# Output projection two slots later, moments of x two slots earlier, batch 1's conv taps two slots later, and the last batch's y projected block by block

## What is computed

```python
# layer 0: Mamba block, d_inner 512, 16 states, conv of 4 taps
xn = layernorm(x) * (1 + scale) + shift
x_in, z = split(xn @ in_proj)
u = silu(conv4(x_in)); dt_r, B, C = split(u @ x_proj); dt = softplus(dt_r @ dt_proj + b)
h[t] = h[t-1] * exp(dt[t] * A) + (dt[t] * u[t]) * B[t]      # a scan over t for 512 x 16 rows
y = (sum_n h * C + u * D) * silu(z)
x = x + gate * (y @ out_proj)
# layer 1: linear attention, 8 heads of 32
q, k, v = rows of layernorm(x);  q = softmax over a head's 32;  k = softmax over time, masked
att = k^T v per head;  y = q att
x = x + silu(layernorm(y) * (1 + scale) + shift) @ W_out + b_out
```

## Time and profile before

| | |
|---|---|
| median of 3 runs | 592.57 us (592.15, 592.57, 598.32) |
| the profiled execution | 598.08 us, its span 596.3 us |
| VectorE busy | 525.1 us, 88% of the span |
| TensorE, GpSimd, ScalarE busy | 76%, 73%, 68% |
| mean granted TensorE clock | 0.86 |
| chain that ended last | VectorE 44%, GpSimd 17%, TensorE 15%, issue 13%, ScalarE 8% |

### The profile page before, as it was taken

The page is one execution under the profiler, slowest core; times in us unless marked ns, Lnnn a source line. Parts: engine busy times, 40 slices in busy tenths (PEclk is TensorE's granted clock), DMA queues, the critical chain, the costliest instruction groups (busy, mean ns, idle before and its releaser), DMA issues.

```text
span 596.3 us, 7355 instructions
## 1 busy us (share of the span) xinstructions
PE 455.0 (76%) x2445; PEld 370.4 (62%) x2445; DVE 525.1 (88%) x576; ACT 405.8 (68%) x885; POOL 436.2 (73%) x311
## 2 busy tenths in 40 slices
PE   8987756678677868779686868789776878657877
PEld 6656545457564757658574757667674767546755
DVE  2377999999999899999999999999999998899533
ACT  3673868588965977497856977497856976675242
POOL 4069779959976899577976899577977899683010
PEclk9977767889899788889789878879789877798988
DMA  9192034013310144003310143003300143000001
GB/s 269 50 353 59 18 143 140 3 28 125 125 35 1 38 168 124 1 27 127 125 52 1 44 162 124 0 28 143 124 35 10 34 153 117 1 18 1 0 1 36
DMA packets 22366, 45.38 MB, mean 76 GB/s; under 512 B 3684, under 2 KB 13556, under 8 KB 22328
## 3 DMA queue, kind: packets, MB, share of 16 engines
q1 hardware_dynamic: 22328, 44.92, 22.4%
HBM read 42.52 MB, written 2.39 MB: 75 GB/s over the span
## 4 chain that ended last, share of the span: by engine, by line
DVE 44%; POOL 17%; PE 15%; issue 13%; ACT 8%; DMA 2%; SPq 0%; DVEq 0%; ACTq 0%; POOLq 0%
DVE ring L855 22%; POOL hs L507 11%; DVE hs L855 6%; DVE hs L862 4%; DVE conv L830 4%; PE sums L1199 3%; ACT ring L667 3%; PE PY L1247 2%; POOL hs L516 2%; PE sums L1081 2%; DMA Br<-bc_rows 1%; PE PX L1147 1%; DVE st L810 1%; DVE ygT L869 1%; ACT L608 1%
## 5 line engine op out<-in xcount | busy, mean ns | idle before, releaser
L507 POOL TENSOR_TENSOR hs<-dtu,Br 128x1024 f32<-128x1024 f32 x127 | 296.3, 2359 | 8.9 <-DMA Br<-bc_rows 8.9
L667 ACT ACTIVATE ring<-dt,Aneg 128x256 f32<-128x256 f32 x512 | 213.1, 465 | 90.5 <-DVE hs L862 87.7
L855 DVE TENSOR_TENSOR_SCAN ring<-ring,hs 128x1024 f32<-128x1024 f32 x104 | 237.0, 2279 | 6.2 <-ACT ring L667 6.2
L1199 PE MATMUL sums<-ident,hs 128*128 128x128 f32 x1024 | 150.1, 303 | 37.1 <-DVE hs L862 36.9
L1199 PEld LDWEIGHTS sums<-ident,hs 128*128 128x128 f32 x1024 | 135.2, 159 | 53.0 <-DVE hs L862 49.1
L862 DVE TENSOR_TENSOR hs<-ring,Cr 128x1024 f32<-128x1024 f32 x104 | 127.3, 1224 | 3.6
L516 POOL TENSOR_TENSOR hs<-hs,Cr 128x1024 f32<-128x1024 f32 x24 | 56.6, 2358 | 56.1 <-DVE hs L855 56.1
L1247 PE MATMUL PY<-wqkvo,xT 128*128 128x256 f32 x168 | 57.8, 506 | 0.0
L855 DVE TENSOR_TENSOR_SCAN hs<-ring,hs 128x1024 f32<-128x1024 f32 x24 | 54.7, 2279 | 0.0
L1247 PEld LDWEIGHTS PY<-wqkvo,xT 128*128 128x128 f32 x168 | 44.9, 267 | 9.9
L591 ACT ACTIVATE conv<-PX,par 128x256 f32<-128x256 f32 x30 | 15.3, 559 | 52.1 <-PE PX L1147 51.9
(11 more groups left out here) (196 smaller groups left out, 670.4 us busy)
## 6 DMA issues: line engine op xcount, KB each, us to landing
Br<-bc_rows SPq DMA_DIRECT2D x32, 512.0 KB, 5.0
Cr<-bc_rows SPq DMA_DIRECT2D x32, 512.0 KB, 4.0
xg<-in_x SPq DMA_DIRECT2D x8, 256.0 KB, 2.8
out<-fin SPq DMA_DIRECT2D x7, 256.0 KB, 4.3
hs<-in_ada_wT SPq DMA_DIRECT2D x3, 512.0 KB, 4.7
win<-in_in_wT SPq DMA_DIRECT2D x2, 512.0 KB, 6.1
hs<-in_W_emb SPq DMA_DIRECT2D x2, 512.0 KB
gate<-gate_rows SPq DMA_DIRECT2D x8, 128.0 KB, 3.0
```

The lines of the kernel that those rows point to most:

```text
L507: nc.gpsimd.tensor_tensor(hs[:, g % DBUF], dtu[:, b % 2, dc, :].unsqueeze(1).to_broadcast([P, NQ, T]), Br[:, NQ * q:NQ * q + NQ, :], ALU.m ...
L667: ins = nc.scalar.activation(ring[:, g % 2, j, :], dt[:, b % 2, dc, :], ACT.Exp, scale=Aneg[:, c:c + 1])
L855: V.tensor_tensor_scan(driven if by_pool(g) else decays, decays, driven, 0.0, ALU.mult, ALU.add).then_inc(s_scan_done, 1)
L1199: ins = M(YT[:, c, :], hs[:, g % DBUF, j, P * c:P * c + P], ident[:, :], is_transpose=True, start=False, stop=(q == UPC - 1 and j == NQ - ...
```

## The change

It does five things, in the order of the program.

1. `conv_taps` 0 and 1 of batch 1 on VectorE, `conv_last_tap` 1 on ScalarE and `in_proj` 1, 2 and 3 on TensorE are due two slots later (`due_later`). All other batches keep their slots.
2. `stats0` is due in slot 7 of an earlier batch (-25) where it was in slot 9 (-23).
3. `output` is due in slot 7 (39), ahead of `x_proj`, where it was in slot 5 (37).
4. The last y is transposed back, copied and projected by blocks of 128 channels: blocks 0 to 2 during slots 10 to 15 (`last_back`, `last_yg`, `last_early`), through `PX`, and only block 3 after unit 127.
5. In the end part: VectorE does `last_x1` for both halves before batch 6's `head_blocks`, `normalize_q` and `stats2`; batch 6's attention on TensorE comes after the last projection of y; the transposed k goes to `PX` ahead of v and is copied by ScalarE; the head sums come after k times v; ScalarE's table load stands after the copy of q; batch 6's transposes move behind the head sums. GpSimd's queue is unchanged.

```diff
+def due_later(g, slot):
+    if g == U + slot + 2:
+        return 1
+    b = due(g, slot)
+    return None if b == 1 else b
...
+            def last_yg(dcs, bank):
+                n = len(dcs)
+                act.wait_ge(s_last_yback, dcs[-1] + 1)
+                act.wait_ge(s_out_mm, LAST_B)
+                nc.scalar.activation(yg[:, dcs[0]:dcs[0] + n, :], bank[:, 0:n, :], ACT.Copy).then_inc(s_last_yg, n)
+            def last_copy_kT():
+                act.wait_ge(s_kT_mm, NB)
+                nc.scalar.activation(kT[:, :, :], PX[:, :, :], ACT.Copy).then_inc(s_kT_ready, 1)
...
                 copy_kT(LAST_B - 1)
-                copy_yg(LAST_B)
+                last_yg((3,), z_bank(LAST_B))
                 last_normalize1(0)
-                normalize2(LAST_B - 1)
                 last_normalize1(1)
                 norm1(LAST_B)
+                normalize2(LAST_B - 1)
                 exp_k(LAST_B)
+                last_copy_kT()
                 exp_q(LAST_B)
-                nc.scalar.preload_act_table_set("silu_and_others")
                 mask_v(LAST_B)
                 copy_qT(LAST_B)
+                nc.scalar.preload_act_table_set("silu_and_others")
...
+                if g == LAST_B * U + 13:
+                    last_yg((0, 1), PX)
+                if g == LAST_B * U + 15:
+                    last_yg((2,), PX)
...
                 gate_y(LAST_B, DC - 1)
+                last_x1(0)
+                last_x1(1)
                 head_blocks(LAST_B - 1)
                 normalize_q(LAST_B - 1)
                 stats2(LAST_B - 1)
-                last_x1(0)
-                last_x1(1)
                 max_qk(LAST_B)
                 sum_k(LAST_B)
-                dve.wait_ge(s_kT_mm, NB)
-                V.tensor_copy(kT[:, :, :], y_bank(LAST_B)[:, :, :]).then_inc(s_kT_ready, 1)
...
-                for slot, step in ((-23, stats0), ...
+                for slot, step in ((-25, stats0), ...
-                    b = due(g, slot)
+                    b = (due_later if step in (conv_taps_0, conv_taps_1) else due)(g, slot)
...
+            def last_back(dcs, bank, until):
+                pe.wait_ge(s_ygT_ready, DC * LAST_B + until)
+                for i, dc in enumerate(dcs):
+                    for c in range(TC):
+                        ins = nc.tensor.transpose(bank[:, i, P * c:P * c + P], ygT[:, c, P * dc:P * dc + P], ident[:, :])
+                ins.then_inc(s_last_yback, len(dcs))
+            def out_part(c, dcs):
+                for k in dcs:
+                    ins = M(last_half(c), yg[:, k, P * c:P * c + P], wo[:, k, :], start=(k == 0), stop=(k == DC - 1),
+                            skip_group_check=True)
+                return ins
+            def last_early():
+                pe.wait_ge(s_last_yg, 3)
+                for c in range(TC):
+                    out_part(c, (0, 1, 2))
...
-                                   (-13, in_proj_3), (-9, x_proj), ...
+                                   (-13, in_proj_3), (39, output), (-9, x_proj), ...
-                                   (35, transpose_y), (37, output)):
-                    b = due(g, slot)
+                                   (35, transpose_y)):
+                    b = (due_later if step in (in_proj_1, in_proj_2, in_proj_3) else due)(g, slot)
...
+                if g == LAST_B * U + 10:
+                    pe.wait_ge(s_vabs_ready, 2 * NB)
+                    last_back((0, 1), PX, 2)
+                if g == LAST_B * U + 13:
+                    pe.wait_ge(s_last_yg, 2)
+                    last_back((2,), PX, 3)
+                if g == LAST_B * U + 14:
+                    last_early()
```

More of the change, by code:

```diff
@@ L288, in build @@
         s_out_stored = sem("out_stored")
+        s_last_yback = sem("last_yback")
+        s_last_yg = sem("last_yg")
+        s_last_heads = sem("last_heads")
         s_last_added = sem("last_added")
@@ L793, in _ @@
                                    (33, copy_kT), (38, normalize2)):
-                    b = (due_soon if step is normalize0 else due)(g, slot)
+                    b = (due_soon if step is normalize0 else due_later if step is conv_last_tap_1 else due)(g, slot)
                     if b is not None:
@@ L1059, in _ @@
                         gate_y(b, dc)
-                for slot, step in ((-23, stats0), (-16, conv_taps_0), (-14, conv_taps_1), (21, gate_x),
+                for slot, step in ((-25, stats0), (-16, conv_taps_0), (-14, conv_taps_1), (21, gate_x),
                                    (22, stats1), (27, max_qk), (30, sum_k), (32, head_blocks), (33, normalize_q),
                                    (34, stats2), (40, finish)):
-                    b = due(g, slot)
+                    b = (due_later if step in (conv_taps_0, conv_taps_1) else due)(g, slot)
                     if b is not None:
@@ L1285, in head_sums @@
                         lo = HEADS * c + HEADS // KD * h
-                        M(k_bank(b)[:, 1, lo:lo + HEADS // KD], qT[:, h, P * c:P * c + P], blockmask[:, 0::DH], start=True,
-                          stop=True)
+                        ins = M(v_bank(b)[:, 0, lo:lo + HEADS // KD] if b == LAST_B else PZ[:, 1, lo:lo + HEADS // KD], qT[:, h, P * c:P * c + P], blockmask[:, 0::DH], start=True,
+                                stop=True)
+                return ins
             def k_times_v(b):
                 pe.wait_ge(s_kT_ready, b + 1)
-                pe.wait_ge(s_qT_ready, b + 1)
-                head_sums(b)
+                if b < LAST_B:
+                    pe.wait_ge(s_qT_ready, b + 1)
+                    head_sums(b)
                 for h in range(KD):
@@ L1327, in last_steps @@
                 y, z, v, k = y_bank(b), z_bank(b), v_bank(b), k_bank(b)
-                transpose_back(b)
+                last_back((3,), z, DC)
+                pe.wait_ge(s_last_yg, DC)
+                for c in range(TC):
+                    out_part(c, (3,)).then_inc(s_out_mm, 1)
                 k_times_v(b - 1)
[L1330 to L1333, removed]
                 for h in range(KD):
@@ L1347, in last_steps @@
                 bias_rows(y, 0)
-                pe.wait_ge(s_yh_ready, TC * b)
-                transposes(PZ, xh).then_inc(s_yT_mm, 1)
+                keep_on(4)
                 pe.wait_ge(s_xT_ready, KD * NB)
@@ L1358, in last_steps @@
                 ins.then_inc(s_q_mm, 1)
+                pe.wait_ge(s_ke_ready, KD * NB)
+                transposes(PX, ke).then_inc(s_kT_mm, 1)
                 for c in range(TC):
@@ L1368, in last_steps @@
                 k_times_v(b)
-                keep_on(4)
+                pe.wait_ge(s_qT_ready, NB)
+                head_sums(b).then_inc(s_last_heads, 1)
+                pe.wait_ge(s_yh_ready, TC * b)
+                transposes(PZ, xh).then_inc(s_yT_mm, 1)
                 pe.wait_ge(s_att_ready, KD * NB)
@@ L1412, in _ @@
                 for slot, step in ((17, transpose_back), (19, out_proj), (-19, transpose_x), (-18, in_proj_0), (-16, in_proj_1), (-14, in_proj_2),
[L1413 removed]
+                                   (-13, in_proj_3), (39, output), (-9, x_proj), (-8, dt_proj_0), (-6, dt_proj_1),
                                    (23, transpose_x1), (24, q_and_k),
                                    (28, v_rows), (29, transpose_qk), (31, k_times_v), (31, q_times_att),
[L1416 to L1417 removed]
+                                   (35, transpose_y)):
+                    b = (due_later if step in (in_proj_1, in_proj_2, in_proj_3) else due)(g, slot)
                     if b is not None and not (b == LAST_B - 1 and step in (k_times_v, q_times_att)):
                         step(b)
+                if g == LAST_B * U + 10:
[6 more added lines that the diff above has]
+                    last_early()
                 if g == -2:
```

17 lines of the change are left out of this document (10 added, 7 removed).

## The result

| | before | after |
|---|---|---|
| median | 593.8 us (20 runs, 589.48 to 598.34) | 591.17 us (20 runs, 586.82 to 592.72) |
| ratio to before | | 0.9944 [0.9919, 0.9969] |
| the profiled execution, its span | 598.08, 596.3 us | 592.20, 590.4 us |
| mean granted TensorE clock | 0.86 | 0.89 |

The change makes the kernel 0.56% faster by the ratio, some 3.3 us (the two medians are 2.6 apart; the ratio compares executions on the same chip). The forecast was 7.5 us and 1.3%. 591.17 lies inside the range, 6.1 above the forecast.

The account below looks back on a forecast made before the run. VectorE, busy 96% from 120 to 530 us, was taken to bound the kernel. Start -1.9, moments -3.4, output projection -2.6 and end +0.4 gave -7.5, set against the median 592.57: 585.1 us, range 581.5 to 591.2.

Parts of the forecast that it names:

- Moments and output: Loop: moving x's moments to slot 7 saves 3.4 us, moving the output projection to slot 7 saves 2.6 us.
- waits for decays: Loop: VectorE waits 4.7 us, five times, for ScalarE's decays; moved moments fill all but one wait of 1.0.
- waits for sums: Loop: VectorE waits 3.1 us, three times, for TensorE's sums; moving the output projection removes them.
- the taps: Start: moving batch 1's taps later gains 0.4 to 1.7 us at unit 8.
- it starts at 62.9 to 64.2 ... against 64.85 before: Start: when unit 6 starts on VectorE, after 2.1 to 3.4 us idle, compared with the old order.
- the 1.5 us before unit 2: Start: VectorE idles 1.5 us before unit 2, waiting for ScalarE's decays.
- the stall: Start: VectorE idles 2.1 to 3.4 us before unit 6, whose decays stand behind copy_z, which waits for z's projection.
- only ScalarE's waits are lasting: Rival: the median execution has no waits hanging on TensorE's clock; 4.3 us saved, 588.3 us; chance 0.20.
- the end: End part: y by blocks and the new order lose 0.4 us, between 0.5 gained and 6.4 lost.
- the prediction's full-clock bound: End part: with TensorE at full clock, 0.5 us gained.
- The end eats the gain: Rival, end part: x1's normalisation behind batch 6's and low clock in both places lose 6.4 us; 591.1 us; chance 0.10.
- Slower: Rival, loop: the output projection runs at half clock in every batch, 12.6 us lost; 597.2 us; chance 0.06.

Follow-up runs that it names:

- moments_output: The kernel before with only the moments of x and the output projection moved (parts 2 and 3); 587.46 us, ratio 0.9884.
- only_end: The kernel before with only the end part changed (parts 4 and 5); 594.16 us, ratio 1.0008.
- only_taps: The kernel before with only batch 1's taps and projections two slots later (part 1); 594.86 us, ratio 1.0004.
- only_moments: The kernel before with only the moments of x moved from slot 9 to slot 7 (part 2); 588.06 us, ratio 0.9914.
- kept_on: The full change with 40 instead of 10 unused matmuls in TensorE's idle time in the end part; 589.56 us, ratio 0.9901.
- no_taps: The full change with batch 1's taps where they were (without part 1); 590.15 us, ratio 0.9908.
- copy_later: The full change with batch 1's copy_z one slot later in ScalarE's queue; 588.59 us, ratio 0.9883.
- only_output: The kernel before with only the output projection moved from slot 5 to slot 7 (part 3); 591.01 us, ratio 0.9964.
- x1_first: The full change with GpSimd's normalisations of the last x1 ahead of batch 6's rstd2; 584.67 us, ratio 0.9826.
- no_taps_x1: The full change without part 1 and with GpSimd's normalisations of the last x1 ahead of batch 6's rstd2; 580.77 us, ratio 0.9766.

## Why the prediction was wrong

**What was right.** The bound (VectorE, idle in few places) and the loop as a sum. Moments and output were to save 3.4 + 2.6, and 0.9 at the start: 6.9. moments_output measured 6.9 (0.9884 of 593.8; interval 4.0 to 9.9); that the two agree to a tenth is luck, given that interval. From unit 10 to unit 127 its trace has 464.8 us, against 472.7, 472.9 and 470.5 in the three with the old loop (before, only_end, only_taps). The mechanism of the one was right: waits for decays 4.7 to 1.0. The other half was put down to the wrong part. The 3.1 us of waits for sums go with the moments alone, which shorten TensorE's idle ahead of the output projection. In only_moments the loop's busy time is all that both reach, so the two terms overlap, and the 2.6 wasn't `output`'s own.

**The step that failed: the taps.** It reads "it starts at 62.9 to 64.2 ... against 64.85 before". The new side held as a sum: unit 8 comes 37.14 us after unit 0, where the forecast had 37.1 to 38.4. That is partly luck, since the 1.5 us before unit 2 didn't come and the stall is 3.86 us for 2.1 to 3.4, with z's projection at 3.78 where 1.98 or 3.31 was allowed. The other side of the subtraction was wrong. The 64.85 comes from one execution in which the stretch of the first taps ran at a clock of 0.61, with waits of 2.28 and 3.31. With the same order and a clock of 1.00 these are 0.23 and 0, and unit 8 comes 33.35 after unit 0. Like against like, both with a first projection of 3.78, the gain at unit 8 is the 0.5 (38.80 to 38.34) that lies in the forecast's 0.4 to 1.7: the step is right for the execution it was read from and not for the others. The term of -1.0 for the taps is +2.4 to +2.9 by the traces with 1.99, and -0.5 to 0 by those with 3.78; by the times it is 0 ± 2 alone (1.0004) and +2.1 within the change (0.9944 against 0.9908, whose intervals overlap). The prediction did say that shorter executions may lack some of the waits, and it had a rival for this, "only ScalarE's waits are lasting"; but that one still left 0.4 of gain here. No case of it had the old waits gone and the new one there, which is a loss.

**The term that was mis-sized: the end.** Its steps came in order and near their marks: x1 at 5.19 (5.06), first xhat at 14.84 (14.56), k to last y 8.05 (8.05). One didn't: the low clock after the idle was given 0.6 us and cost 2.3. The last y is 1.6 later than before and not 0.4. kept_on takes just that away and ends 0.7 ahead of before, where the prediction's full-clock bound was 0.5 ahead (its own sum without the 0.6 gives 0.2). The size differs between executions: with the same 3.95 us of idle k took 2.79, 3.68, 3.68 and 3.78 us in four traces (only_end, no_taps, copy_later, after), and the last y started at 28.8, 30.0, 29.9 and 30.2. By the times the end costs 1.4 (0.9908 against 0.9884) to 2.0 (0.9944 against 0.9911), and 0.5 ± 2.3 alone (1.0008).

**The sum.** -6.9 (moments, output) + 1.6 (taps) + 2.0 (end), or, in the other order, -6.9 + 1.4 (end) + 2.1 (taps): -3.3 or -3.4, measured -3.3. These are differences of measured ratios from one kernel to the next, so they must add up; they share the loss out and prove nothing, and each is good to 2 or 3 us only. The forecast's -7.5 had -6.9 - 1.0 + 0.4. Both errors lie in how TensorE's clock was priced: the old start was taken at the low clock of one execution, and the end was allowed 0.6 us for a low clock that cost 2.3.

**The rivals.** "Only ScalarE's waits are lasting" (588.3) is nearer for the old start and wrong for the loop: the waits for sums stood there in every trace of the old loop, 3.1 us each, and went. "The end eats the gain" gives 591.1, and 591.17 was measured, but that is luck: its end was to lose 6.4 at half clock in both places, and the early projection ran at full clock (2.6 us). "Slower" did not occur: from 120 to 530 us there was one wait of 1.1 for `output`.

**Open.** How often the first taps' projection runs at half clock: it took 3.78 us in five of the 14 traces (before, only_taps, only_output, x1_first, no_taps_x1). They aren't only long executions: the one of x1_first (584.61 us) is at its median. The setup before unit 0 took 34.2 to 35.1 us in four traces (before, no_taps_x1, x1_first, only_end), three of them of the five, and 36.1 to 37.1 in the others. What decides isn't shown. Nor is it shown why TensorE's idle ahead of the output projection is shorter with the moments moved.

## What to carry to other kernels

A wait that ends at a matmul has two sizes, one at each clock. Before its removal is counted as a gain, price the stretch once with the matmuls at their full-clock duration, for the old order too, and count only what is left. When work on the critical path is moved forward on one engine, look at the in-order queue of every engine after it: here one swap in GpSimd's queue was worth 7 us, and without it the last y came 1.6 later. Two waits in the same slots may be no separate terms: the waits for decays and for sums both went with one step. Undo them one at a time before adding them.

## What the runs showed of the hardware

The same eight records of a projection, after the same 2.52 us idle of TensorE, took 3.78 us in one execution (before) and 1.99 in another (only_end), and units 0 to 10 of unchanged code 46.8 and 41.7 us. Thirty more matmuls that nobody uses, 0.11 us apiece (kept_on), bought back 2.3 us of the end's path.
